# Decoder layer on one core: scores and transposed scores of the steady attention steps issued in pairs, at 8 places instead of 20

## The chip, the cores and the metric

The kernel runs on one core of a Trainium2 chip. The metric is the device time of one execution in microseconds (us); the number compared is the median of several runs.

## What is computed

A post-norm decoder layer on x (2 batches, 512 tokens, 1024 features, f32):

```python
qkv = x @ attn_qkvw + attn_qkvb                    # 32 heads of 32
scores = einsum('bhqd,bhkd->bhqk', q, k) / sqrt(32)
ctx = einsum('bhqk,bhkd->bhqd', softmax(scores), v)
x = layernorm(x + ctx @ attn_ow + attn_ob)
x = layernorm(x + matmul(fake_quant(x), fake_quant(ctx_4096)))
x = layernorm(x + (x @ W_base.T + b_base + experts(x)))    # top 2 of 8 LoRA experts
```

The change touches the first line group alone: projections, scores, softmax and context.

## The kernel before

**Units and steps.** The attention is cut into 16 units: one group of 4 heads in one batch. A unit's q, k and v projections are 24 groups of 3 matmuls each (`project`, L524; 3 because an f32 product is made of a high and a low part, `split_mm`, L466). A unit's scores are 16 tiles of 128 queries by 512 keys (`score`, L554), needed only for the maximum and the sum of each row; then 16 tiles of the transposed scores, 128 keys by 512 queries (`score_t`, L585), with the maxima already subtracted inside the product; their exponentials are the probabilities that `context` (L598) multiplies with v.

**Three units in flight.** Step s projects unit s, makes the scores and row maxima of unit s-1, and the transposed scores and the context of unit s-2. Steps 3 to 15 do all three with the same program ("steady"; steps 4 to 13 are a loop of pairs). Step 1 (`second`) and step 2 (`third`) have tables of their own; steps 16 and 17 use other functions.

**The order on TensorE is written by hand.** One loop over q = 0 to 47 (L661) issues a projection group at each even q, and `score(n)` and `score_t(n)` at the q that `score_slot(n)` (L197) and `transposed_slot(n)` (L201) give. In steady steps the scores stand at 2, 5, 8, 10, 13, 15, 18, 20, 23, 25, 28, 30, 33, 35, 38, 40, and the transposed ones at 2, 5, 8, ... 47. Since projections come at even q only, this gives 20 places between projection groups where something of the 32 tiles stands: 12 with one tile of each kind and 8 with a single tile. Two transposes of small tiles stand at q = 6 (`recip_to_rows`, L576) and q = 45 (`maxima_to_rows`, L568). After the loop comes `context()`, and the next step begins with four transposes of v (`transpose_v`, L512).

**Who follows.** Scores use three PSUM banks in turn, transposed scores two. VectorE takes the maximum of each score tile (L1385); ScalarE then makes the exponential of the tile with its row sums (`exp_sum`, L865; L868). ScalarE makes the exponential of each transposed tile (`exp_scores`, L857; L863). `score(n)` waits for `exp_sum(n-3)`, `score_t(n)` for `exp_scores(n-2)`. The order on ScalarE is a loop over q of its own (L872): `exp_scores(n)` one slot after its tile, `exp_sum(n)` three slots after its tile. VectorE goes through n = 0 to 15; between its maxima it copies the row of reciprocals (after n = 2), splits q (`low(0)`, L1336, after n = 5; L1343 and L1346), clips the other input (`clip_context`, L1350, after n = 8; L1355), splits k (`low(1)`, after n = 11) and rounds (`round_context`, L1357, after n = 13). After the maxima of a step a row of them is copied to SBUF and the SP queue stores it into qp (`store_shift`, L294), for which the first `score_t` of the next step waits. The SP queue also copies the split q and k into qp and kp (`pack`, L242).

Of the kernel before, what the change touches and what calls it, by code (L numbers as in the profile page):

```python
# [6 lines left out]
def decoder_layer(nc, xT, x, wqkv, qkvb, ow, ob, ctx_in, scales, wbT, bb, art, bt, out):  # L7
# [20 lines left out]
    NS = HPG * QT  # L28
# [15 lines left out]
    with es:  # L44
# [142 lines left out]
        def stages(s):  # L187

            if not isinstance(s, int):
                return True, True, True  # L190
            return s < UNITS, 1 <= s <= UNITS, s >= 2
# [4 lines left out]

        def score_slot(n, second):  # L197

            return 6 + (34 * n + 14) // 15 if second else 2 + (38 * n + 14) // 15

        def transposed_slot(n, third):  # L201

            return 8 + (39 * n + 14) // 15 if third else 2 + 3 * n

        def raw_home(n):

# [2 lines left out]
        def max_bank(s, n):  # L209

            return MAX[1 - n % 2] if isinstance(s, int) and s == UNITS else MAX[n % 3]
# [7 lines left out]
        def bank(i, lo=0, hi=512):  # L219
            return banks[i][:, lo:hi]  # L220
# [244 lines left out]
        def _(pe):  # L465
# [41 lines left out]
            def step(s, par, g):  # L507
                proj, maxima, finish = stages(s)
                first = isinstance(s, int) and s == 0
                second = isinstance(s, int) and s == 1  # L510

                def transpose_v():  # L512

                    pe.wait_ge(sem["vT_ok"], s)
                    pe.wait_ge(sem["lo_ok"], 2 * s)
                    if not isinstance(s, int) or s >= 2:
                        pe.wait_ge(sem["m_ok"], s - 1)
                    if isinstance(s, int) and s == 1:
                        pe.wait_ge(sem["const_ok"], 1)
                    for t in range(QT):  # L520
                        mm = nc.tensor.transpose(bank(PROJ0, t * P, (t + 1) * P), vT[:, t * P:(t + 1) * P], ident[:, :])  # L521
                    mm.then_inc(sem["vt_mm"], 1)
# [31 lines left out]
                def score(n):  # L554

                    j, t = n // QT, n % QT
                    if t == 0:
                        pe.wait_ge(packed[j], PACK_INC * s)
                    if n >= 2 and isinstance(s, int) and s == UNITS:
                        pe.wait_ge(sem["sum_ok"], NS * (s - 1) + n - 1)  # L560
                    elif n >= 3:
                        pe.wait_ge(sem["sum_ok"], NS * (s - 1) + n - 2)
                    elif n == 0 and (not isinstance(s, int) or s >= 2):
                        pe.wait_ge(sem["sum_ok"], NS * (s - 1))
                    nc.tensor.matmul(bank(max_bank(s, n)), qp[0:SHIFT, 1 - par, j, t * P:(t + 1) * P],  # L565
                                     kp[0:SHIFT, 1 - par, j, :], start=True, stop=True).then_inc(sem["max_mm"], 1)

                def maxima_to_rows():  # L568
                    pe.wait_ge(sem["rowmax"], NS * s)
                    if proj:  # L570
                        pe.wait_ge(sem["lo_ok"], 2 * s + 2)
                    else:
                        pe.wait_ge(sem["r_row_ok"], s - 1)
                    nc.tensor.transpose(banks[rows_bank(s)][0:NS, 0:P], m_col[:, :], ident[:, :]).then_inc(sem["m_mm"], 1)

                def recip_to_rows():  # L576

                    pe.wait_ge(sem["r_ok"], s - 1)
                    if not maxima:
                        pe.wait_ge(sem["m_ok"], s - 1)  # L580
                    elif divides(s):
                        pe.wait_ge(sem["ctx_ok"], s - 2)
                    nc.tensor.transpose(banks[CTX][0:NS, P:2 * P], r_col[:, :], ident[:, :]).then_inc(sem["r_mm"], 1)

                def score_t(n):  # L585

                    j, t = n // QT, n % QT
                    if n == 0:
                        pe.wait_ge(sem["shift_in"], 32 * (s - 1))
                        if isinstance(s, int) and s == 2:  # L590
                            pe.wait_ge(sem["plus_ok"], 1)
                            pe.wait_ge(sem["vT_ok"], 2)
                    if n >= 2:
                        pe.wait_ge(sem["exp_ok"], NS * (s - 2) + n - 1)
                    nc.tensor.matmul(bank(ST0 + n % 2), kp[0:SHIFT + 2, par, j, t * P:(t + 1) * P],  # L595
                                     qp[0:SHIFT + 2, par, j, :], start=True, stop=True).then_inc(sem["st_mm"], 1)
# [63 lines left out]
                done, turned, third = 0, 0, isinstance(s, int) and s == 2  # L660
                for q in range(3 * NS):  # L661
                    if early and q == KT:
                        transpose_v()
                    if proj and q % 2 == 0:
                        project(q // 2)
                    if maxima and done < NS and q == score_slot(done, second):
                        score(done)
                        done += 1
                    if maxima and q == 3 * NS - 3:
                        maxima_to_rows()  # L670
                    if finish and turned < NS and q == transposed_slot(turned, third):
                        score_t(turned)
                        turned += 1
                    if finish and q == 6:
                        recip_to_rows()
                if finish:
# [163 lines left out]
        def _(act):  # L840
            def split_x(b, ks):

                for k in ks:
                    act.wait_ge(big_in[b][k], 32 - 16 * b)
                    nc.scalar.activation(big_hi[:, b, k], big_raw[:, b, k], ACT.Identity).then_inc(sem["x_hi_ok"], 1)
# [7 lines left out]
            def step(s, par, g):  # L853
                proj, maxima, finish = stages(s)
                prev = not isinstance(s, int) or s >= 1

                def exp_scores(i):  # L857

                    j, t = i // QT, i % QT
                    act.wait_ge(sem["st_mm"], NS * (s - 2) + i + 1)  # L860
                    if i == 0 and (not isinstance(s, int) or s >= 3):
                        act.wait_ge(sem["pv_mm"], s - 2)
                    nc.scalar.activation(probs[:, j, t, :], bank(ST0 + i % 2), ACT.Exp).then_inc(sem["exp_ok"], 1)  # L863

                def exp_sum(n):  # L865

                    act.wait_ge(sem["rowmax"], NS * (s - 1) + n + 1)
                    nc.scalar.activation(bank(max_bank(s, n)), bank(max_bank(s, n)), ACT.Exp, bias=m_col[:, n:n + 1],  # L868
                                         accum_out=l_col[:, 1 - par, n:n + 1]).then_inc(sem["sum_ok"], 1)

                done, turned, third = 0, 0, isinstance(s, int) and s == 2
                for q in range(3, 3 * NS + 3):  # L872
                    if finish and turned < NS and q == transposed_slot(turned, third) + 1:
                        exp_scores(turned)
                        turned += 1
                    if maxima and done < NS and q == (score_slot(done, isinstance(s, int) and s == 1) + 3 if proj else 3 * done + 3):
                        exp_sum(done)
                        done += 1
                    if isinstance(s, int) and s == 0 and q in (16, 33):
                        split_x(1, range(5) if q == 16 else range(5, KT))  # L880
                def pack_first_keys(j):

                    rows = slice(j * HD, (j + 1) * HD)
                    for row, src in ((0, k_hi), (PACK_HI2, k_hi), (PACK_LO, k_lo)):
                        act.dma_start(kp[row:row + HD, 0, j, :].bitcast(f32), src[rows, :].bitcast(f32)).then_inc(packed[j], 16)

                if not prev:
                    act.wait_ge(sem["lo_ok"], 2)
                    pack_first_keys(0)
                    pack_first_keys(1)  # L890
                if proj:
                    act.wait_ge(sem["proj_done"], 3 * s + 3)
                    if not prev:
                        act.wait_ge(sem["scale_q"], 1)
                    if prev:
                        wait_alone(act, sem["vt_mm"], s)
                    nc.scalar.activation(vT[:, :], bank(ST0 if isinstance(s, int) and s <= 1 else PROJ1), ACT.Identity,
                                         bias=bias[:, bass.ds(g, 1), 2:3].rearrange("p a b -> p (a b)")).then_inc(sem["vT_ok"], 1)
# [846 lines left out]
```

## Time and profile before

| | us |
|---|---|
| median of 3 runs | 728.88 (728.86 to 729.34) |
| profiled execution, its own time | 729.37 |
| span of the profiled execution | 727.6 |
| TensorE (PE) busy | 703.4 (97%) |
| VectorE (DVE) busy | 470.0 (65%) |
| ScalarE (ACT) busy | 426.1 (59%) |
| GpSimd (POOL) busy | 279.6 (38%) |

The span is the time between the first and the last instruction that the profile shows; 1.8 us of the execution's own time lie around it. L469 is the line in the helper where every split matmul is recorded, L565 a score tile, L595 a transposed one, L609 the context, L521 and L574 transposes. PEld is the weight load that belongs to each matmul.

### The profile page before, as it was taken

Reading aid. Unit: us, or ns where it says so; the run is one execution under the profiler, and the core shown is the slowest. Engines: PE = TensorE matmul, PEld = TensorE weight load, DVE = VectorE, ACT = ScalarE, POOL = GpSimd, SP = SyncE. Lnnn points to the kernel's source line nnn. Section 1 sums busy time; section 2 is a strip of 40 time slices with the busy share of each in tenths; the row PEclk is TensorE's granted clock in tenths of the full one; section 3 lists DMA queues with packets and bytes.
Section 4 is the critical chain, followed back from the end, with each engine's and each line's share of the span. In section 5 each row is a group of like instructions: output and inputs, shape, how many; then the busy total and the mean of one; then the engine's idle time right before and its main releaser. Section 6 shows DMA issues by size and latency. Waiting matters only on the chain.

```text
span 727.6 us, 11766 instructions
## 1 busy us (share of the span) xinstructions
PE 703.4 (97%) x3477; PEld 526.5 (72%) x3484; DVE 470.0 (65%) x831; ACT 426.1 (59%) x919; POOL 279.6 (38%) x206
## 2 busy tenths in 40 slices
PE   6989999999999999999999999999999997999996
PEld 5868668668677686686686776758667765788884
DVE  5887557466476575574575665467678787665564
ACT  5458668667686685686776866853656662211111
POOL 5573250270171162153143168644725643111111
PEclk9999999999999999999999999999999999999999
DMA  8666436436426336335344277718542603131101
GB/s 289 177 187 217 114 82 200 118 78 206 124 69 199 102 94 196 88 109 172 111 116 124 70 230 222 248 61 285 193 144 88 217 17 117 62 110 60 59 29 59
DMA packets 55732, 98.97 MB, mean 136 GB/s; under 512 B 10896, under 2 KB 21392, under 8 KB 54800
## 3 DMA queue, kind: packets, MB, share of 16 engines
q1 hardware_dynamic: 55408, 98.13, 43.7%
q10 hardware_dynamic: 288, 0.39, 0.2%
q8 instruction: 18, 0.29, 0.2%
q14 instruction: 18, 0.15, 0.1%
HBM read 56.41 MB, written 16.65 MB: 100 GB/s over the span
## 4 chain that ended last, share of the span: by engine, by line
PE 64%; issue 16%; DVE 7%; POOL 7%; DMA 2%; ACT 2%; SPq 2%; POOLq 0%; DVEq 0%; ACTq 0%
PE bank L469 39%; PE bank L595 8%; PE bank L609 8%; PE bank L565 8%; POOL xb L1205 2%; SPq L253 2%; DVE st L1459 1%; POOL mv L1186 1%; POOL x1s L1192 1%; PE bank L521 1%; POOL wb_lo L1197 1%; DMA w_raw<-in_wqkv 1%; DMA xres<-in_x 1%; DVE wb_lo L1517 1%; DVE x1s L1506 1%
## 5 line engine op out<-in xcount | busy, mean ns | idle before, releaser
L863 ACT ACTIVATE probs<-bank 128x512 f32<-128x512 f32 x256 | 152.2, 597 | 118.3 <-PE bank L595 115.1
L1385 DVE TENSOR_REDUCE m_col<-bank 128x1 f32<-128x512 f32 x256 | 172.7, 687 | 75.1 <-PE bank L565 74.4
L868 ACT ACTIVATE bank<-bank,m_col 128x512 f32<-128x512 f32 x256 | 169.2, 661 | 18.5 <-DVE m_col L1385 16.7
L469 PE MATMUL bank<-big_hi,w_hi 128*128 128x512 f32 x384 | 156.6, 408 | 6.3 <-DVE big_lo L1280 6.3
L469 PE MATMUL bank<-big_lo,w_hi 128*128 128x512 f32 x384 | 152.5, 397 | 0.0
L469 PE MATMUL bank<-big_hi,w_lo 128*128 128x512 f32 x384 | 151.2, 394 | 0.0
L565 PE MATMUL bank<-kp,qp 96*128 96x512 f32 x256 | 101.3, 396 | 0.7 <-ACT bank L868 0.7
L595 PE MATMUL bank<-qp,kp 98*128 98x512 f32 x256 | 101.0, 398 | 0.0
L469 PEld LDWEIGHTS bank<-big_hi,w_hi 128*128 128x128 f32 x384 | 73.3, 191 | 24.9 <-DVE big_lo L1280 6.3
L469 PEld LDWEIGHTS bank<-big_hi,w_lo 128*128 128x128 f32 x384 | 72.8, 190 | 17.0
L469 PEld LDWEIGHTS bank<-big_lo,w_hi 128*128 128x128 f32 x384 | 73.5, 192 | 14.8
L1131 POOL TENSOR_SCALAR c_raw<-c_raw,sc 128x1024 f32<-128x1024 f32 x16 | 19.3, 1206 | 144.9 <-DMA c_raw<-in_ctx 141.4
L1186 POOL TENSOR_TENSOR mv<-mv,consts 128x1 f32<-128x1 f32 x24 | 15.9, 662 | 139.0 <-DVE mv L1467 132.6
L1108 POOL TENSOR_TENSOR c_sum<-c_sum,c_q 128x1024 f16<-128x1024 f16 x16 | 34.3, 2144 | 87.6 <-DVE c_q L1362 87.6
L609 PE MATMUL bank<-probs,v_nat 128*32 128x512 f32 x512 | 58.2, 595 | 0.0
L565 PEld LDWEIGHTS bank<-kp,qp 96*128 96x128 f32 x256 | 48.1, 188 | 13.0 <-ACT bank L868 1.6
L595 PEld LDWEIGHTS bank<-qp,kp 98*128 98x128 f32 x256 | 48.3, 189 | 12.6 <-ACT probs L863 1.6
L469 PE MATMUL bank<-wb_hi,x2T_hi 128*128 128x512 f32 x128 | 51.7, 404 | 2.3 <-DVE wb_lo L1517 2.3
L469 PE MATMUL bank<-big_hi,cx_hi 128*128 128x512 f32 x128 | 51.8, 405 | 0.0
L1371 DVE COPY v_nat<-bank 128x512 f32<-128x512 f32 x16 | 11.0, 690 | 62.8 <-PE bank L521 62.8
L868 ACT ACTIVATION_READ_ACCUMULATOR bank<-bank,m_col 128x1 f32 x256 | 51.3, 200 | 0.0
L1075 POOL TENSOR_TENSOR w_lo<-w_raw,w_hi 128x1024 fp32r<-128x1024 f32 x21 | 50.5, 2406 | 1.8
(139 smaller groups left out, 1101.7 us busy)
## 6 DMA issues: line engine op xcount, KB each, us to landing
w_raw<-in_wqkv SPq DMA_DIRECT2D x7, 1536.0 KB, 8.1
c_raw<-in_ctx SPq DMA_DIRECT2D x16, 512.0 KB, 4.1
qp<-q_hi SPq DMA_DIRECT2D x128, 64.0 KB, 2.0
kp<-k_hi SPq DMA_DIRECT2D x124, 64.0 KB, 2.0
big_raw<-in_xT SPq DMA_DIRECT2D x16, 256.0 KB, 5.7
qp<-q_lo SPq DMA_DIRECT2D x64, 64.0 KB, 2.0
c_scratch<-c_q SPq DMA_DIRECT2D x16, 256.0 KB, 2.2
r_all<-r_scratch SPq DMA_DIRECT2D x64, 64.0 KB, 2.0
```

The source lines that it names most:

```text
L253: sp.dma_start(dst[row:row + HD, par, j, :].bitcast(f32), src[rows, :].bitcast(f32)).then_inc(packed[j], 16)
L469: mm = nc.tensor.matmul(dst, lhs[a], rhs[b], start=(k == 0 and n == 0) if first is None else False, stop=(k == last_k and n == 2))
L565: nc.tensor.matmul(bank(max_bank(s, n)), qp[0:SHIFT, 1 - par, j, t * P:(t + 1) * P], kp[0:SHIFT, 1 - par, j, :], start=True, stop=True).th ...
L595: nc.tensor.matmul(bank(ST0 + n % 2), kp[0:SHIFT + 2, par, j, t * P:(t + 1) * P], qp[0:SHIFT + 2, par, j, :], start=True, stop=True).then_ ...
L609: mm = nc.tensor.matmul(banks[context_bank(s - 2)][j * HD:(j + 1) * HD, :], v_nat[:, par, t, j * HD:(j + 1) * HD], probs[:, j, t, :], star ...
L863: nc.scalar.activation(probs[:, j, t, :], bank(ST0 + i % 2), ACT.Exp).then_inc(sem["exp_ok"], 1)
L868: nc.scalar.activation(bank(max_bank(s, n)), bank(max_bank(s, n)), ACT.Exp, bias=m_col[:, n:n + 1], accum_out=l_col[:, 1 - par, n:n + 1]). ...
L1075: nc.gpsimd.tensor_tensor(w_lo[:, piece], w_raw[:, piece], w_hi[:, piece].bitcast(f32), ALU.subtract).then_inc(sem["w_split"], 1)
L1108: nc.gpsimd.tensor_tensor(c_sum[:, b], c_sum[:, b], c_q[:, :], ALU.add).then_inc(sem["ctx_added"], 1)
L1131: nc.gpsimd.tensor_scalar(c_raw[:, :], c_raw[:, :], sc[:, 6:7], sc[:, 3:4], ALU.mult, ALU.add).then_inc(sem["ctxq_1"], 1)
L1186: nc.gpsimd.tensor_tensor(mv[:, row, 2:3], mv[:, row, 1:2], consts[:, 0:1], ALU.pow).then_inc(sem[ok], 1)
L1385: nc.vector.reduce_max(m_col[:, n:n + 1], bank(max_bank(s, n)), AX, negate=True).then_inc(sem["rowmax"], 1)
```

## The change

In steps 3 to 15 both kinds of tile get the same table: tiles 2m and 2m+1 of both stand together at q = 2, 7, 12, 18, 23, 29, 34, 40, and the loop body runs twice there, so that each place has score, transposed, score, transposed. In step 2 the scores alone move to these places, in pairs, and the transposed keep their table. On ScalarE `exp_sum` now has its turn at slot + 1, the same as `exp_scores`, and the two alternate. Steps 0, 1, 16 and 17 keep their order.

```diff
         def score_slot(n, second):
 
-            return 6 + (34 * n + 14) // 15 if second else 2 + (38 * n + 14) // 15
+            return 6 + (34 * n + 14) // 15 if second else 2 + 38 * (n // 2) // 7
 
         def transposed_slot(n, third):
 
-            return 8 + (39 * n + 14) // 15 if third else 2 + 3 * n
+            return 8 + (39 * n + 14) // 15 if third else 2 + 38 * (n // 2) // 7
...
                     if proj and q % 2 == 0:
                         project(q // 2)
-                    if maxima and done < NS and q == score_slot(done, second):
-                        score(done)
-                        done += 1
+                    for _ in range(2):
+                        if maxima and done < NS and q == score_slot(done, second):
+                            score(done)
+                            done += 1
+                        if finish and turned < NS and q == transposed_slot(turned, third):
+                            score_t(turned)
+                            turned += 1
                     if maxima and q == 3 * NS - 3:
                         maxima_to_rows()
-                    if finish and turned < NS and q == transposed_slot(turned, third):
-                        score_t(turned)
-                        turned += 1
...
                 for q in range(3, 3 * NS + 3):
-                    if finish and turned < NS and q == transposed_slot(turned, third) + 1:
-                        exp_scores(turned)
-                        turned += 1
-                    if maxima and done < NS and q == (score_slot(done, isinstance(s, int) and s == 1) + 3 if proj else 3 * done + 3):
-                        exp_sum(done)
-                        done += 1
+                    for _ in range(2):
+                        if finish and turned < NS and q == (transposed_slot(turned, third) + 1 if proj else 3 * turned + 3):
+                            exp_scores(turned)
+                            turned += 1
+                        if maxima and done < NS and q == (score_slot(done, isinstance(s, int) and s == 1) + 1 if proj else 3 * done + 3):
+                            exp_sum(done)
+                            done += 1
```

## Rows read from the trace of the kernel before

**Rows 1.** The page: TensorE's busy tenths and granted clock, 40 slices.
```profile
PE   6989999999999999999999999999999997999996
...
PEclk9999999999999999999999999999999999999999
```
**Rows 2.** Busy time per engine, five steady steps from context to context.
```profile
sum 143.00, PE 143.00 PEld 104.70 DVE 88.30 ACT 101.21 POOL 47.48; mean PE 28.60 PEld 20.94 DVE 17.66 ACT 20.24 POOL 9.50
```
**Rows 3.** All waits of L565 in the whole span, by releaser.
```profile
PE bank L565 <- ACT bank L868: 0.7, 1, 0.7
```
**Rows 4.** TensorE in order of time (start, duration in us), a place of two tiles.
```profile
295.81 0.39 PE L565 MATMUL bank<-kp,qp 96*128 96x512 f32 x1
...
296.28 0.40 PE L469 MATMUL bank<-big_hi,w_hi 128*128 128x512 f32 x1
...
296.98 0.39 PE L469 MATMUL bank<-big_hi,w_hi 128*128 128x512 f32 x1
...
297.66 0.40 PE L565 MATMUL bank<-kp,qp 96*128 96x512 f32 x1
```
**Rows 5.** TensorE in a long run without scores (output projection).
```profile
492.96 0.39 PE L469 MATMUL bank<-big_hi,cx_lo 128*128 128x512 f32 x1
...
493.87 0.39 PE L469 MATMUL bank<-big_hi,cx_hi 128*128 128x512 f32 x1
```
**Rows 6.** TensorE, a place of one tile.
```profile
287.42 0.39 PE L565 MATMUL bank<-kp,qp 96*128 96x512 f32 x1
287.65 0.40 PE L469 MATMUL bank<-big_hi,w_hi 128*128 128x512 f32 x1
...
288.35 0.39 PE L565 MATMUL bank<-kp,qp 96*128 96x512 f32 x1
```
**Rows 7.** The end of a steady step on TensorE.
```profile
301.72 0.40 PE L595 MATMUL bank<-qp,kp 98*128 98x512 f32 x1
302.05 0.64 PE L609 MATMUL bank<-probs,v_nat 128*32 128x512 f32 x4
```
**Rows 8.** All engines in order of time around two tiles and what follows them.
```profile
288.35 0.19 PEld L595 LDWEIGHTS bank<-qp,kp 98*128 98x128 f32 x1
...
288.58 0.40 PE L595 MATMUL bank<-qp,kp 98*128 98x512 f32 x1
...
289.01 0.60 ACT L863 ACTIVATE probs<-bank 128x512 f32<-128x512 f32 x1 [0.82 <-PE bank L595]
...
289.51 0.66 ACT L868 ACTIVATE bank<-bank,m_col 128x512 f32<-128x512 f32 x1
289.51 0.40 PE L565 MATMUL bank<-kp,qp 96*128 96x512 f32 x1
...
289.95 0.69 DVE L1385 TENSOR_REDUCE m_col<-bank 128x1 f32<-128x512 f32 x1 [0.23 <-PE bank L565]
...
290.08 0.20 ACT L868 ACTIVATION_READ_ACCUMULATOR bank<-bank,m_col 128x1 f32 x1
290.17 0.66 ACT L868 ACTIVATE bank<-bank,m_col 128x512 f32<-128x512 f32 x1
```
**Rows 9.** VectorE in order of time: the q split and the clip of a steady step.
```profile
257.39 0.69 DVE L1385 TENSOR_REDUCE m_col<-bank 128x1 f32<-128x512 f32 x1 [0.48 <-PE bank L565]
258.17 0.75 DVE L1343 TENSOR_SCALAR q_hi<-bank,bias 128x512 fp32r<-128x512 f32 x1
259.07 0.75 DVE L1346 SCALAR_TENSOR_TENSOR q_lo<-bank,bias,q_hi 128x512 fp32r<-128x512 f32 x1
259.73 1.28 DVE L1385 TENSOR_REDUCE m_col<-bank 128x1 f32<-128x512 f32 x2
...
261.95 1.79 DVE L1355 TENSOR_SCALAR c_raw<-c_raw 128x1024 f32<-128x1024 f32 x1
263.67 1.40 DVE L1385 TENSOR_REDUCE m_col<-bank 128x1 f32<-128x512 f32 x2
```
**Rows 10.** The SP queue at the end of a steady step: the maxima's store.
```profile
302.30 1.22 SPq L298 DMA_DIRECT2D qp<-m_row  x2
```

## The prediction

> **What bounds the kernel now.** I read the page first: TensorE is busy in nine tenths or more of nearly every slice and its granted clock is full, that is 2.4 GHz, throughout [rows 1]. So the question is only what stands between its matmuls. Then the busy times step by step: five steady steps, cut at the start of the context, last 28.60 us each, TensorE is busy for all of it, and ScalarE for 20.24 and VectorE for 17.66 [rows 2]. Nothing else is near the bound. The table of waits has a single wait of a score on an exponential in the whole span, 0.7 us [rows 3], and in the order of time it lies in step 16, which the change leaves alone. In the steady steps, then, TensorE never waits for what the change reorders; the reordering can take time out only through the distance from one matmul's start to the next.
>
> That distance isn't constant. Deep in a long run of projection matmuls four starts take 493.87 - 492.96 = 0.91, or 0.227 each [rows 5]. Around a place with scores it is longer: two tiles and the group of three behind them take 296.98 - 295.81 = 1.17 for five, 0.234 each; the group alone takes 0.70, and the next group, which follows a group and not a score, 297.66 - 296.98 = 0.68 [rows 4]. A single tile and its group take 288.35 - 287.42 = 0.93 for four [rows 6]. So a place costs, over 0.227 a matmul, 1.17 - 1.135 = 0.035 with two tiles and 0.93 - 0.908 = 0.022 with one.
>
> **The change, part by part.** Nothing is added to or taken from the work: 32 tiles, 72 projection matmuls, two small transposes and the context as before. The places go from 20 (12 with two tiles, 8 with one) to 8 with four tiles.
>
> TensorE, first way, by places. Before: 12 x 0.035 + 8 x 0.022 = 0.60 us a step. A place of four is nowhere in the trace; I take the first tile at 0.022 and each further at the 0.013 by which two exceed one, 0.061. After: 8 x 0.061 = 0.49. Gain 0.11 us a step. Second way, by groups: a group behind a group takes 0.68 instead of 0.70. Leaving out the first two groups of the step and the ones behind the two transposes, which don't change, before only two groups of a step follow a group (q = 38 and 44); after, 13 do (q = 6, 10, 12, 16, 18, 22, 26, 28, 32, 34, 38, 40, 44). 11 x 0.02 = 0.22 us a step. Both rest on differences of 0.01 to 0.02, about the rounding of the rows, so I take the middle, 0.165. Bounds: no gain at all, if each score tile costs its own excess wherever it stands; and 0.22. The whole 0.60 can't go, since the tiles keep their waits.
>
> Thirteen steps (3 to 15) have the new table: 13 x 0.165 = 2.1 us, between 13 x 0.11 = 1.4 and 13 x 0.22 = 2.9. In step 2 the count of places goes from 22 to 20 only, since the transposed keep their table: 0.04, nothing.
>
> ScalarE, same operations in another order. Relative to T, the start of a place's first matmul, the tiles start at T, T+0.23, T+0.47 and T+0.70. An exponential starts 289.01 - 288.58 = 0.43 after its tile's start, holds ScalarE for 0.50 and is over after 0.60; a maximum starts 289.95 - 289.51 = 0.44 after its tile's start and takes 0.69; the exponential with its sum holds ScalarE for 290.17 - 289.51 = 0.66, and its sum is read out 290.28 - 289.51 = 0.77 after its start [rows 8]. So exp_scores(a) starts at T+0.66, the maximum of a is ready at T+1.13 and exp_sum(a) starts at T+1.17, its sum is out at T+1.95, exp_scores(a+1) runs from T+1.85 to T+2.45, exp_sum(a+1) from T+2.35 and ScalarE is free at T+3.03. The next place stands four matmuls and two or three groups later: 0.93 + 1.40 = 2.33 (from 2 to 7 and from 18 to 23; the first has the transpose of q = 6 as well) or 0.93 + 2.10 = 3.03. What it needs: the fourth tile needs exp_scores(a+1). Its weights load when the matmul before it starts, as L595's at 288.35 with its matmul at 288.58 [rows 8], and that load carries the wait: it is due at T+2.33+0.47 = T+2.80 at the earliest. It is there at T+2.45, 0.35 ahead. The third tile needs exp_sum(a), out at T+1.95, due at T+2.56. ScalarE's work of a place, 2 x (0.50 + 0.66) = 2.32, fits the shorter distance. So the new waits cost nothing; their cover is 0.35 us.
>
> VectorE: its other operations stand between the same n, and now behind tiles that come two at once. The q split follows maximum 5 (place 12) and waits for the group at q = 14, whose last matmul ends at T+0.93+0.47+0.40 = T+1.80; with the 0.15 or so that the chain of semaphores takes (258.17 - 257.39 is 0.78 where two maxima stand 0.60 to 0.64 apart), it begins near T+1.98, q_lo 0.90 later and the next maximum 0.66 after that [rows 9], at T+3.54, where tile 6 is ready at T+3.03+0.44 = T+3.47. So maximum 6 is 0.07 late, and this is the place (18) before a short distance: the cover falls to 0.28. The clip behind maximum 8, up to 1.72 in the queue [rows 9], delays exp_sum(9) to T+3.5, exp_scores(11) then ends at T+5.95, due at T+6.53: 0.58 left. The k split behind maximum 11 makes maximum 12 some 0.17 late before a long distance: free.
>
> The end of the step. The last transposed tile moves from q = 47 to 40, so the context's first wait is older; the 0.33 between the last matmul and the first of the context [rows 7], 0.10 over a normal start, I leave as it is, since the context's own waits and its f32 matmuls stay. The last maximum is ready at T+1.73 of place 40; the transpose of q = 45 needs it at about T+2.10. The store of the maxima goes out on the SP queue behind the copies of q and k, at 302.30 [rows 10], when the context has just begun; the context, four transposes, two projection groups and a score still stand before the first transposed tile, which waits for it. The k split, which sets when those copies go, follows the group of q = 30 as before. What is queued on SP behind it (copies for heads 2 and 3) is first used in the middle of the next step. GpSimd waits for projection groups, which keep their order.
>
> After step 15 everything shifts as a whole: TensorE bounds steps 16 and 17 as before.
>
> **The sum.** Span 727.6 - 2.1 = 725.5; with the 1.8 around it 727.3 for an execution like the profiled one, whose 729.37 lies 0.5 above the median of 728.88. Against that median: 726.8 us. A measurement of this kernel can tell about 0.2% (1.46 us) from no change.
>
> **The rivals.** A: the excess belongs to each score tile, not to the place. Two tiles cost more than one [rows 4, 6], so a part of it surely does; if all of it does, four cost 4 x 0.022 a place, 8 x 0.088 = 0.70, against 0.60 before, and the time is 728.9 to 730; with the tiles' share anywhere near that it stays within 0.2%. [...] Against A stands that 0.68 directly behind the 0.70, with the same operands, in the same step [rows 4]. Chance of no difference, 0.29, for this and for gains too small to see.
>
> B, slower: the cover at place 23 is too thin. Maximum 6 sits behind the q split; if that comes 0.6 us later than I work out (one VectorE operation more, or a copy of q and k still landing, for which it also waits), then exp_sum(6) and exp_scores(7) behind it on the same engine come 0.6 late, and the fourth tile of place 23 waits 0.6 - 0.28 = 0.32 us. The point from which it decides is 0.28. Thirteen times: 4.2 - 2.1 = +2.1 us, 731.0. For it: ScalarE is in order, and the change takes away the three slots by which exp_sum used to stand behind its tile. Against it: every term above comes from a row, and both engines have a quarter of the step free. Chance 0.13.
>
> C: four tiles in a row disturb no more than two do, and the groups behind settle at once: 0.22 a step or a little more, 726.0 to 725.4. This is the good end of my forecast. Forecast and C together 0.58. That the change doesn't do what it says is excluded: the tables are plain.
>
> The range: 725.4 takes in C, with the rounding of the rows; 729.4 takes in A; B is left out, about 0.12, and a little on either side.
>
> **What would show it.** Steady steps of 28.4 instead of 28.6 us, TensorE busy for all of it; places of four followed by groups of 0.70, 0.69 or 0.68, 0.68; no wait of L595 on L863 or of L565 on L868 in steps 3 to 15. Were A right, the step would be 28.6 with the second groups at 0.70 or the four tiles over 0.95. Were B right, the fourth tile of place 23 would start late by tenths. The forecast is wrong if the steps differ by under 0.1 or if any stall appears.

## The result, and the profile after

The changed kernel is slower: 731.13 us (9 runs) beside 728.74 us of the kernel before, ratio 1.0037 (1.0025 to 1.0049). Run again, beside 728.93 us of the kernel before, it was 730.90 us, ratio 1.0032 (1.0018 to 1.0047). The ratios, here and below, are those of the fast executions and not the quotients of the medians, from which they differ by up to 0.0008. The forecast was 726.8, in a range from 725.4 to 729.4.

The page hardly moves, with TensorE full as in [rows 1]:

```profile
span 729.3 us, 11766 instructions
PE 705.7 (97%) x3477; PEld 525.4 (72%) x3484; DVE 464.3 (64%) x831; ACT 425.3 (58%) x919; POOL 279.7 (38%) x206
```

Where [rows 2] had 28.60 us for every steady step, the same view, cut at the transpose of the maxima, shows the steps alternating:

```profile
303.72:332.32 28.60, 28.60 (x144) 20.81 (x143) 18.06 (x28) 20.06 (x51) 11.22 (x8) 1.00 0.39 102
332.32:361.02 28.70, 28.70 (x144) 20.81 (x143) 16.58 (x28) 20.15 (x51) 6.84 (x5) 1.00 0.50 156
```

No gain of 0.165 a step, it seems, and TensorE "busy" throughout. But the waits of the weight loads now name the exponentials (us in total, times, longest; the first two lines are of the kernel before, the last two of the changed one):

```profile
PEld bank L595 <- ACT probs L863: 1.6, 8, 0.3
PEld bank L565 <- ACT bank L868: 1.6, 3, 1.1
...
PEld bank L595 <- ACT probs L864: 6.1, 22, 0.7
...
PEld bank L565 <- ACT bank L869: 3.6, 8, 1.2
```

Between 75 and 470 us, where the steady steps are, the changed kernel has 13 waits of L595, 3.8 us in all, as many as there are steady steps, and the kernel before has none. [Rows 3] were the waits of the matmuls; in that view the changed kernel has a single one of L595, 0.3 us. A tile carries its wait on its weight load, and there it has to be looked for.

(The new code lies 1 line lower on ScalarE and 2 on VectorE: L864 is the old L863, L869 the old L868, L1387 the old L1385.) The order of time at a place of four, first one without a wait, then the one at q = 23:

```profile
290.31 0.40 PE L565 MATMUL bank<-kp,qp 96*128 96x512 f32 x1
290.54 0.40 PE L595 MATMUL bank<-qp,kp 98*128 98x512 f32 x1
290.78 0.40 PE L565 MATMUL bank<-kp,qp 96*128 96x512 f32 x1
291.01 0.40 PE L595 MATMUL bank<-qp,kp 98*128 98x512 f32 x1
291.25 0.39 PE L469 MATMUL bank<-big_hi,w_hi 128*128 128x512 f32 x1
...
291.95 0.39 PE L469 MATMUL bank<-big_hi,w_hi 128*128 128x512 f32 x1
...
292.63 0.40 PE L565 MATMUL bank<-kp,qp 96*128 96x512 f32 x1
292.86 0.40 PE L595 MATMUL bank<-qp,kp 98*128 98x512 f32 x1
293.10 0.44 PE L565 MATMUL bank<-kp,qp 96*128 96x512 f32 x1
293.53 0.50 PE L595 MATMUL bank<-qp,kp 98*128 98x512 f32 x1
293.86 0.40 PE L469 MATMUL bank<-big_hi,w_hi 128*128 128x512 f32 x1
```

Place 18 takes 291.25 - 290.31 = 0.94 for its four tiles, and the group behind the first group 0.68 again: the gain is there. Place 23 takes 293.86 - 292.63 = 1.23. In this step 0.29 us is lost at one place; in the steps between it is about 0.2. What the fourth tile waits for, in the same step on all engines:

```profile
287.31 0.40 PE L565 MATMUL bank<-kp,qp 96*128 96x512 f32 x1
...
289.92 0.75 DVE L1345 TENSOR_SCALAR q_hi<-bank,bias 128x512 fp32r<-128x512 f32 x1 [0.89 <-PE bank L469]
...
290.82 0.75 DVE L1348 SCALAR_TENSOR_TENSOR q_lo<-bank,bias,q_hi 128x512 fp32r<-128x512 f32 x1
...
291.49 1.28 DVE L1387 TENSOR_REDUCE m_col<-bank 128x1 f32<-128x512 f32 x2
292.21 0.66 ACT L869 ACTIVATE bank<-bank,m_col 128x512 f32<-128x512 f32 x1 [0.63 <-DVE m_col L1387]
...
292.89 0.59 ACT L864 ACTIVATE probs<-bank 128x512 f32<-128x512 f32 x1
...
293.04 0.19 PEld L565 LDWEIGHTS bank<-kp,qp 96*128 96x128 f32 x1 [0.21 <-ACT bank L869]
...
293.52 0.19 PEld L595 LDWEIGHTS bank<-qp,kp 98*128 98x128 f32 x1 [0.30 <-ACT probs L864]
```

This is rival B. The q split starts 2.61 us after place 12 (287.31) instead of 1.98, maximum 6 starts 1.18 after place 18 (290.31) instead of 0.51, and exp_scores(7) behind exp_sum(6) ends at 293.48. The third tile's load is late too (293.04, behind exp_sum(6)), but the last to end is the wait of the fourth: its weights could have loaded at 293.10; it starts at 293.53 instead of 293.33, and the matmul behind it another 0.1 late.

The second loss is in step 2, to which the forecast had given nothing. From the maxima's transpose of step 1 to that of step 2 the profiles have 45.95 to 71.88 = 25.9 us before and 46.10 to 74.90 = 28.8 us after (26.9 in the repeated run). In the order of time, after the change:

```profile
49.45 1.42 DVE L1364 TENSOR_SCALAR c_q<-c_raw,consts 128x1024 bf16<-128x1024 f32 x1
50.79 0.23 DVE L1325 RECIPROCAL r_col<-l_col 128x16 f32<-128x16 f32 x1
50.94 1.81 DVE L1387 TENSOR_REDUCE m_col<-bank 128x1 f32<-128x512 f32 x3
51.07 0.09 PEld L583 LDWEIGHTS bank<-ident,r_col 128*16 128x16 f32 x1 [1.21 <-DVE r_col L1325]
...
51.60 0.66 ACT L869 ACTIVATE bank<-bank,m_col 128x512 f32<-128x512 f32 x1 [3.70 <-DVE m_col L1387]
...
52.43 0.19 PEld L565 LDWEIGHTS bank<-kp,qp 96*128 96x128 f32 x1 [1.16 <-ACT bank L869]
```

VectorE comes out of step 1 with the clip and the rounding of the other input and starts the maxima of step 2 at 50.94 (at 51.36 in the kernel before). score(3), now at q = 7 with three banks in turn, needs exp_sum(0), which waits for that first maximum. The wait for r_col just before it is not new: it was 1.8 us in the kernel before.

In this execution the granted clock then fell to half, 1.2 GHz, in step 2: behind the two waits, in which TensorE sat idle for 0.77 us before 51.08 and 0.85 us before 52.43, its matmuls start 0.43 us apart from 53.9 to 56.0. The columns are busy us by engine, granted clock, DMA share and GB/s:

```profile
50.00:60.00 10.00, 8.38 (x32) 6.40 (x31) 6.25 (x11) 5.47 (x15) 5.07 (x3) 0.83 0.71 213
```

0.17 of 10 us is 1.7 us at full clock that the stretch did not have. The repeated run and e2, e3, e6 and e9 below had the same wait of 1.2 us for exp_sum(0) in their profiles and no such stretch.

### The profile page after: what moved, and what is told of

Its sections match the earlier page's. It is cut to its first block, busy times and chain, and to the rows that moved or that the text cites. A ratio compares the mean times of both kernels' runs of the same rounds, so it can differ in the third digit from the quotient of the medians.

```text
span 729.3 us, 11766 instructions
## 1 busy us (share of the span) xinstructions
PE 705.7 (97%) x3477; PEld 525.4 (72%) x3484; DVE 464.3 (64%) x831; ACT 425.3 (58%) x919; POOL 279.7 (38%) x206
## 4 chain that ended last, share of the span: by engine, by line
PE 69%; issue 15%; DVE 7%; POOL 3%; ACT 3%; DMA 2%; SPq 1%; ACTq 0%; POOLq 0%; DVEq 0%
PE bank L469 41%; PE bank L595 9%; PE bank L565 8%; PE bank L609 8%; POOL xb L1207 2%; PE bank L721 1%; PE bank L521 1%; DVE st L1461 1%; DMA big_raw<-in_xT 1%; DVE quant L1493 1%; SPq L227 1%; POOL mv L1188 1%; DMA kp<-k_lo 1%; DVE x1s L1508 1%; DVE m_col L1387 1%
## 5 line engine op out<-in xcount | busy, mean ns | idle before, releaser
L1387 DVE TENSOR_REDUCE m_col<-bank 128x1 f32<-128x512 f32 x256 | 167.5, 684 | 74.2 <-PE bank L565 73.4
L864 ACT ACTIVATE probs<-bank 128x512 f32<-128x512 f32 x256 | 152.1, 598 | 102.1 <-PE bank L595 100.7
L869 ACT ACTIVATE bank<-bank,m_col 128x512 f32<-128x512 f32 x256 | 169.7, 663 | 35.0 <-DVE m_col L1387 34.6
L469 PE MATMUL bank<-big_hi,w_hi 128*128 128x512 f32 x384 | 154.6, 402 | 6.2 <-DVE big_lo L1282 5.6
L565 PE MATMUL bank<-kp,qp 96*128 96x512 f32 x256 | 102.8, 404 | 1.7 <-ACT bank L869 1.5
L595 PE MATMUL bank<-qp,kp 98*128 98x512 f32 x256 | 103.2, 406 | 0.3 <-ACT probs L864 0.3
L595 PEld LDWEIGHTS bank<-qp,kp 98*128 98x128 f32 x256 | 48.7, 191 | 15.9 <-ACT probs L864 6.1
L565 PEld LDWEIGHTS bank<-kp,qp 96*128 96x128 f32 x256 | 48.3, 189 | 15.9 <-ACT bank L869 3.6
L869 ACT ACTIVATION_READ_ACCUMULATOR bank<-bank,m_col 128x1 f32 x256 | 52.2, 204 | 0.0
L469 PE MATMUL bank<-big_lo,cx_hi 128*128 128x512 f32 x128 | 50.1, 391 | 0.0
```

Source lines behind the costliest of these rows:

```text
L469: mm = nc.tensor.matmul(dst, lhs[a], rhs[b], start=(k == 0 and n == 0) if first is None else False, stop=(k == last_k and n == 2))
L1387: nc.vector.reduce_max(m_col[:, n:n + 1], bank(max_bank(s, n)), AX, negate=True).then_inc(sem["rowmax"], 1)
```

## The experiments

**e1 and e2: which steps lose?** Step 2 of the changed kernel on its old tables, and the kernel before with step 2 alone on the new ones.

```diff
# e1, on the changed kernel
-        def score_slot(n, second):
+        def score_slot(n, second, third=False):
+            if third:
+                return 2 + (38 * n + 14) // 15
...
-  (score_slot(done, isinstance(s, int) and s == 1) + 1 if proj
+  (score_slot(done, isinstance(s, int) and s == 1, third) + (3 if third else 1) if proj
# e2, on the kernel before
+            if third:
+                return 2 + 38 * (n // 2) // 7
...
-  (score_slot(done, isinstance(s, int) and s == 1) + 3 if proj
+  (score_slot(done, isinstance(s, int) and s == 1, third) + (1 if third else 3) if proj
```

> The changed kernel, with step 2 alone back on the tables of the kernel before (scores at 2, 5, 8, ..., exp_sum three slots behind). Theory 1 (most of the loss is in step 2, where score(3) at q = 7 waits for exp_sum(0), 1.3 us late because VectorE comes late out of step 1; the steady steps come out even, gain against a stall at place 23): the stall behind the q = 6 transpose goes, the transpose of the maxima of step 2 comes at 71.9 us again instead of 74.9, and the time is 728.9 to 729.3, ratio to before 1.0000 to 1.0008. Rival 2 (the loss is in the 13 steady steps): 730.5 to 731, ratio 1.003.

> The kernel before, with step 2 alone on the new table for scores and exp_sum. Theory 1: the wait of score(3) on exp_sum(0) appears, 1.2 to 1.4 us, and the time is 730.0 to 731.5, ratio 1.002 to 1.004; where the idle stretch also costs clock in step 2, up to 1.7 us more. Rival 2: 728.7, ratio 1.000.

The kernel before took 729.26 us beside e1 to e4. e1: 729.45 us, ratio 1.0000 (0.9988 to 1.0012), step 2 is 25.9 us, steady steps mostly 28.60 and 28.70 to 28.72. e2: 730.30 us, ratio 1.0014 (1.0000 to 1.0027; 1.002 to 1.004 was expected), step 2 is 26.4 us, steady steps 28.60, with the wait of score(3), 1.2 us long. Theory 1 holds: the new table gains nothing and loses little in the steady steps, and step 2 loses. In the profiles of all runs, step 2 took 25.3 to 25.9 us with the old table of the scores (six profiles) and 26.4 to 27.3 with the new one (five profiles without the stretch at half clock), about 1.4 more.

**e3, e4, e5: the waits in front of the q split.** `low()` waits for the projection and then, one by one, that the copies of the last step's four heads are done. In nearly every steady step of the profiles the copies have landed when the projection ends (e6 shows one where they haven't); the edit only passes their waits first. Each of these waits is a `wait_alone` (L213): a wait followed by an increment of a counter.

```diff
-                    wait_alone(dve, sem["proj_done"], 3 * s + piece + 1)
                     if not isinstance(s, int) or s >= 1:
                         for h in range(HPG):
                             wait_alone(dve, packed[h], PACK_INC * s)
+                    wait_alone(dve, sem["proj_done"], 3 * s + piece + 1)
```

e3 is this on the changed kernel, e4 this and e1 together, e5 this on the kernel before.

> The changed kernel, with the four waits on packed[h] in low() ahead of the wait on the projection instead of behind it. Theory 3 (the q split starts 0.8 us after its projection because five waits in a row are passed one after the other once the projection is done; that makes maximum 6 and all behind it 0.7 late and stalls the fourth tile of place 23): q_hi starts some 0.6 us earlier, the wait of L595 on L864 at place 23 is gone, the steady step falls from 28.60-28.70 to 28.35-28.45, and the time is 3 us below the changed kernel, 727.5 to 728.5, ratio 0.9985 to 0.9995 (step 2 still costs 1.5 to 2). Rival 4 (the 0.8 us is the latency from the matmul's end to VectorE, whatever the waits): q_hi and the time stay, 731.

> Both edits together: step 2 as before, and the packed waits first. If theories 1 and 3 hold: steady steps of 28.35 to 28.45, no loss in step 2, 725.5 to 726.5, ratio 0.9955 to 0.997, which is below both kernels. If only theory 1 holds 729, if only theory 3 holds 728.

> The kernel before, with the packed waits ahead of the projection wait in low(). Theory 3: nothing here waits for the q split in the steady steps, since maxima 6 and 7 have places of their own and TensorE never waits; q_hi starts no earlier or a few tenths earlier, the steady step stays 28.60 and the time stays, ratio 0.9990 to 1.0010. Rival 5 (the order of these waits is a gain by itself, wherever it stands): 3 us less, ratio 0.996.

e3: 728.01 us, ratio 0.9991 (0.9976 to 1.0005), 3 us below the changed kernel. Every steady distance but the first is the same length (the first, 28.66, still holds the last transposed tile of step 2, at q = 47):

```profile
300.64:329.05 28.41, 28.41 (x143) 20.90 (x142) 18.33 (x28) 20.07 (x51) 11.11 (x7) 1.00 0.40 103
329.05:357.46 28.41, 28.41 (x144) 20.90 (x142) 16.58 (x28) 20.21 (x51) 6.95 (x5) 1.00 0.51 158
```

and q_hi starts 286.06 - 284.00 = 2.06 us after place 12, where the forecast had 1.98; maximum 6 starts 0.62 after place 18:

```profile
284.00 0.40 PE L565 MATMUL bank<-kp,qp 96*128 96x512 f32 x1
...
286.06 0.75 DVE L1345 TENSOR_SCALAR q_hi<-bank,bias 128x512 fp32r<-128x512 f32 x1 [0.34 <-PE bank L469]
286.96 0.75 DVE L1348 SCALAR_TENSOR_TENSOR q_lo<-bank,bias,q_hi 128x512 fp32r<-128x512 f32 x1
287.00 0.40 PE L565 MATMUL bank<-kp,qp 96*128 96x512 f32 x1
...
287.62 1.28 DVE L1387 TENSOR_REDUCE m_col<-bank 128x1 f32<-128x512 f32 x2
```

e4: 726.52 us, ratio 0.9967 (0.9955 to 0.9979), and 726.54 with the same ratio when run again: faster than both kernels. e5: 728.88 us, beside 728.93, ratio 0.9995 (0.9985 to 1.0005), steady steps 28.60: the order of the waits is worth nothing by itself, only where something waits behind them.

**e9: is it a price by wait?** Two of the four ahead, two behind.

> The changed kernel, with two of the four packed waits ahead of the projection wait and two behind it. Theory 3 puts the price at 0.14 us a wait: q_hi starts 0.82 to 0.93 us after the start of the last matmul of the q projection (1.10 to 1.21 with four behind, 0.55 to 0.66 with none), and the fourth tile of place 23 waits 0 to 0.05 where it waited 0.1 to 0.2: steady steps 28.41 to 28.5. If the price is paid once for the change of semaphore and not by wait, q_hi starts at 1.1 to 1.2 and the steps are 28.6 to 28.7.

728.63 us, beside 729.29, ratio 0.9991 (0.9977 to 1.0005). In the steps of the loop, from the start of the last matmul of the q projection to q_hi it is 1.10 to 1.21 us with four waits behind, 0.78 to 0.89 with two and 0.55 to 0.66 with none: 0.32 for the first two taken away and 0.23 for the others. In steps 3, 14 and 15, outside the loop, it is 0.99 to 1.00, 0.77 to 0.78 and 0.55. So it is a price by wait, 0.11 to 0.16 each; whether the wait costs it or the increment that goes with it in `wait_alone`, no run tells. Up to 0.89 the stall is gone and the steady step is 28.39 to 28.41, but for one of 28.78 with a long clip (2.83 us). At 0.99, in steps 3, 14 and 15 of the changed kernel, 0.06 to 0.15 us a step is still lost. So the cover ends between 0.89 and 0.99. On this scale the forecast had q_hi at 1.98 - 1.40 = 0.58 and the point of rival B at 0.58 + 0.28 = 0.86.

**e6: move the place, not the waits.** The changed kernel with q = 24 for 23, so that three groups follow the place behind the q split.

```diff
-  if second else 2 + 38 * (n // 2) // 7
+  if second else (2, 7, 12, 18, 24, 29, 34, 40)[n // 2]
-  if third else 2 + 38 * (n // 2) // 7
+  if third else (2, 7, 12, 18, 24, 29, 34, 40)[n // 2]
```

> The changed kernel with the place at q = 23 moved to q = 24, waits of low() as they are: the short distance of two groups now comes after place 24, not after place 18, whose maxima the q split delays. Theory 3: the stall in the steady step at that place goes, since the fourth tile has 0.70 us more; steady steps of 28.4 in the steps in which the clip takes 0.7 us and up to 0.2 more where it takes 1.8 (exp_sum(9) then delays exp_scores(11)); 1 to 3 us below the changed kernel, ratio 0.999 to 1.002. If the stall is the mere price of four tiles behind two groups, it moves to place 29 in every step and the time stays at 731.

728.33 us, beside 728.93, ratio 0.9991 (0.9979 to 1.0004), as e3. q_hi is as late as in the changed kernel (0.90 us waited for the projection's end), and of the 13 distances from step 2 to step 15 ten are 28.41 and the first 28.66, as in e3. Two are longer, and there tiles do wait: 29.01 with a clip of 2.37 us, and 29.19 in step 15, where q_hi had to wait for a copy of the step before, the other way for it to be late that rival B had named:

```profile
430.30 0.75 DVE L1345 TENSOR_SCALAR q_hi<-bank,bias 128x512 fp32r<-128x512 f32 x1 [2.07 <-DMA kp<-k_lo]
```

So the stall needs both: the late split and only two groups behind it.

**e7: is the gain one of places?** Both kinds on the old table of the scores, 16 places of two, packed waits first.

> 16 places of two tiles: both kinds on the scores' table of before (2, 5, 8, 10, 13, ... 40), exponentials at slot + 1, packed waits first, in steps 3 to 15. By the theory that a matmul group costs 0.02 less behind a group than behind a score, four groups of a step do (q = 18, 28, 38, 44) against two before and thirteen in the changed kernel: the steady step is 28.55 to 28.58, against 28.60 and the 28.41 of the changed kernel with the packed waits first. If the gain came from alternating the two kinds, or from the transposed tiles ending at q = 40, it is 28.41 here too.

One execution alone, 729.3 us; the steps alternate between 28.59 and 28.70, with a single wait of a tile (0.3 us). So neither alternating the kinds nor ending the transposed ones early is the gain. But the count of groups behind groups, the second way of the forecast, fails too, since it promised 0.04; and so does the first way as the forecast priced it, since 16 places of two at 0.035 come to 0.56 instead of 0.60, again 0.04. The distances tell why: the price of a pair is not fixed. With its group it takes 1.162 to 1.165 us in some places and 1.170 to 1.179 in others, and a group behind a group takes 0.68 behind some and 0.69 (234, 235, 225 ns) behind others. In e3 the picture is regular: a place of four and its group take 1.640 us for seven matmuls, 0.053 over 0.227 each (0.061 forecast), and 8 x 0.053 = 0.42 instead of 0.60 accounts for 0.18 of the 0.19 gained. Why pairs differ was not settled.

**e8 and e10: what step 2 loses.** On e3, score(3) of step 2 back to q = 10; then exp_sum(9) of step 2 back to its turn at q = 28 as well.

```diff
# e8
+            if third and n == 3:
+                return 10
# e10, further
-  score_slot(..., third) + 1
+  score_slot(..., third) + (5 if third and done == 9 else 1)
```

> The kernel of e3 (changed, packed waits first), with score(3) of step 2 alone put back from q = 7 to q = 10; all other tiles of step 2 stay on the new table. Theory 1 (what step 2 loses is the wait of score(3) on exp_sum(0)): the 1.3 us wait behind the q = 6 transpose goes, the transpose of the maxima of step 2 comes at 71.9 to 72.2 us instead of 73.1 (a stall of 0.4 us near 64 us, where a transposed tile waits behind the clip, stays), and the time is 1 to 1.3 us below e3, ratio to before 0.997 to 0.998. Rival 6 (VectorE is late there in any order, so the wait moves to the next score): 73.1 us and the time of e3.

730.04 us, beside 729.29, ratio 1.0010 (0.9996 to 1.0023): a miss. The 1.2 us wait of score(3) is gone from the profile, but a later one grew from 0.7 to 1.5, and step 2 is 26.6 us (e3: 27.3, e4: 25.4 and 25.8). The lines lie 2 lower again here:

```profile
60.21 1.20 POOL L1135 TENSOR_SCALAR c_raw<-c_raw,sc 128x1024 f32<-128x1024 f32 x1 [5.44 <-DMA c_raw<-in_ctx]
...
61.44 0.69 DVE L1359 TENSOR_SCALAR c_raw<-c_raw 128x1024 f32<-128x1024 f32 x1 [0.76 <-POOL c_raw L1135]
...
62.77 0.66 ACT L871 ACTIVATE bank<-bank,m_col 128x512 f32<-128x512 f32 x1 [1.28 <-DVE m_col L1389]
...
63.45 1.78 ACT L866 ACTIVATE probs<-bank 128x512 f32<-128x512 f32 x3
64.08 0.19 PEld L597 LDWEIGHTS bank<-qp,kp 98*128 98x128 f32 x1 [1.55 <-ACT probs L866]
```

The chain starts at a load: the other input lands at 60.2, GpSimd scales it, the clip on VectorE waits for that, maximum 9 stands behind the clip, exp_sum(9) waits for it on ScalarE, and with the new turns exp_scores(6) stands behind exp_sum(9). A TensorE that comes there earlier waits longer. The clock takes part as well: 7 of the 12 executions had a mean granted clock of 0.995 instead of 0.997 to 0.999, and these took 730.3 us in the median, the other five 728.1. The profile (727.3 us, 0.998) is of one of the five, so where the clock fell in the seven is not shown.

> The kernel of e8 (packed waits first, score(3) of step 2 at q = 10), with one more thing put back in step 2: on ScalarE exp_sum(9) has its turn at q = 28 as before the change, not at q = 24. Theory 7: what e8 left is one wait of 1.1 us; exp_sum(9) stands in ScalarE's queue ahead of exp_scores(6), and maximum 9 stands on VectorE behind the clip, which waits for GpSimd and that for the load of the other input, landed at 60.2 us. With the exponentials freed from it, the 1.1 us wait of a transposed tile near 64 us goes, step 2 takes 25.3 to 25.9 us from the maxima's transpose of step 1 to its own, as in the kernel before, and the time is that of e4, 726 to 727, ratio 0.996 to 0.998. Rival: TensorE then waits elsewhere in step 2 and the step stays at 26.6, time as e8.

726.96 us, beside 729.02, ratio 0.9972 (0.9961 to 0.9983), the time of e4, and no execution below 0.997 of the clock. The time came out as expected, the profile did not: in the profiled execution (726.1 us) the load landed 2 us later, at 62.4, and step 2 took 26.5 us with several short waits in place of one. Which part of e10's 3 us is waits and which is clock stays open.

**The repeated runs.**

> The changed kernel itself, once more, on the chip and beside the runs of the ones it is compared with here. 731 us, ratio to before 1.003 to 1.004.

> The kernel of e4 (step 2 on its old table, packed waits first) once more, beside the ones of this call: 725.5 to 727, ratio to before 0.9955 to 0.998, 0 to 0.4 us below e8.

730.90 us and 726.54 us.

## Why the prediction was wrong, point by point

- **TensorE bounds the steps, and places cost.** Right. With the stall out of the way (e3, e4, e6, e9) the steady step is 28.41 us, a gain of 0.19 where 0.165 was forecast. That the middle came so near is in part luck: the first way was low (0.11) by its guessed 0.061 for a place of four, where 0.053 was measured, the second high (0.22), and e7 upholds neither as it was priced. The reason given, "since the tiles keep their waits", is not shown either (see the last section).
- **"With the 0.15 or so that the chain of semaphores takes ... it begins near T+1.98."** This is the step that failed. 0.15 is what one wait takes; five stand in a row, and the four behind the projection's add 0.55 us (0.44 outside the loop). q_hi came at T+2.61. The row used, 258.17 - 257.39 [rows 9], hid them: there the last matmul of the q projection had started 1.68 us before q_hi, and the waits were passed while the maximum before was still running, 0.09 us after whose end q_hi starts. Behind a running operation the chain of waits was free, behind the wait that was released last it was paid one by one. With the four ahead, q_hi came at T+2.06.
- **The cover of 0.28 us, and rival B.** The mechanism, the place and the point were right: maximum 6 came 0.74 us late instead of 0.07, and the fourth tile of place 23 waited. B was given 0.13 on the ground that "every term above comes from a row"; that one did not. Its price was 0.32 a step; measured were 0.2 to 0.3, from 28.41 to 28.60 and 28.70. From the maxima's transpose of step 2 to that of step 15 it is 372.0 us before, 372.3 and 372.6 after and 369.5 in e3: a loss of 2.8 to 3.0 us on a gain of 2.5. The changed kernel has one transposed tile more in this distance, 0.25 us, which it has less in the next one (27.65 before, 27.40 after); with that the steady steps come out 0.0 to 0.3 us longer. B's time, 731.0, was met by luck: it had 4.2 - 2.1 us more from the steady steps, which gave 0.3 at most, and 1.4 came from step 2, which B left out.
- **The clip: "0.58 left".** Right in the steps in which the clip takes up to 2.46 us (e8: 28.41), wrong at 2.65 and more: 28.61 instead of 28.41 with 2.65 (e10), 28.78 instead of 28.41 with 2.83 (e9), 28.85 instead of 28.60 with 2.90 (the changed kernel, repeated). The forecast took 1.72 from one row as the longest; the trace it read has one of 2.55.
- **Step 2: "0.04, nothing."** Wrong by about 1.4 us (e1, e2, and e3 beside e4). The step was judged by its number of places and not by its waits, and the timing of a steady step was taken for it. In step 2 VectorE is busy when the step begins, and the clip waits for a load; both were in the trace. This is the larger part of the net loss.
- **A** (the excess goes with the tiles) fell with 28.41. The Trainium skill's page "TensorE: Matmul & The Clock Gate", section "Back-to-back issue gap", gives about 216 ns (N/2.4 + 2.5) for 512 columns as the gap of an isolated matmul and about 131 ns in a stream of weight loads and matmuls. The traces here disagree with both, with 227 ns in a settled run and 228 to 242 ns around the tiles, for 512 columns each; the measurement decides.
- **The end of the step, the SP queue, GpSimd**: nothing of them shows as a wait of TensorE in the steady steps, as said.
- The parts add up to 0.0 to 0.3 us in the steady steps and about 1.4 in step 2, where 2.4 and 2.0 were measured. In the changed kernel's 17 executions three had a clock of 0.996 or less and took 731.1, 734.0 and 735.4 us; without them the medians would be 731.0 and 730.8, so the clock closes 0.2 us at most, and the rest was not settled.

## What to carry to other kernels

When a wait is moved close to its releaser, work out the whole queue in front of the operation that has to come: each wait behind the last one to be released costs (0.11 to 0.16 us here, with its increment), and waits that are long satisfied belong ahead of it. A uniform order in time is worth less than it seems where one interval is shorter than the rest: put the short interval where no engine has extra work. And a step at the ramp of a pipeline has its own late engines and loads; check the change there against its own rows.

## What the runs showed of the hardware

- A matmul of 512 columns started every 0.227 us in a settled run, and every 0.228 to 0.242 us from a score tile on to the third matmul behind the last tile of its place (places beside the small transposes apart), though nothing waited. Four tiles in a row and the group behind them cost 0.053 us over the settled distance, a pair before about 0.035, a single one 0.022: bunching them gained 0.19 us in 28.6. The cause is open. That the tiles carry a wait is not enough for it: the first matmul at q = 16 carries one too (`project`, k = 0), and in e3 the starts there are 285.64, 285.86, 286.09, 286.32, the settled 0.227.
- A chain of waits that were satisfied long before delayed the next operation of VectorE by 0.11 to 0.16 us each behind the wait that was released last (e3, e9), and by nothing that shows behind a running operation (in the loop, q_hi starts 0.08 to 0.19 us after the end of the maximum before it in the kernel before, 0.06 to 0.17 in e5).
- In one profile of six with the 1.2 us wait of score(3) in step 2, a stretch at half clock (1.2 GHz) followed, worth 1.7 us. In the others the granted clock stayed full.
- The last stage, from the first matmul on x2T (L747, L746 before) to the end, which the change doesn't touch, took 141.7 to 141.9 us in three of the fourteen profiles (the changed kernel, e4 repeated, e10) and 143.1 to 143.2 in the others. So single profiles of two kernels can differ by 1.4 us for this alone.
